# Second cross-attention of a two-layer perceiver block: the first key or value unit of a batch moves between the two halves of the value matmuls

## The reference

```
def _L1_xattn_ref(hidden_states, audio_tokens, attention_mask, Wq, bq, Wk, bk, ...):
    q, k, v = proj(hs, Wq, bq, S), proj(at, Wk, bk, T), proj(at, Wv, bv, T)   # 16 heads of 16 channels
    scores = jnp.clip(jnp.einsum('bhsd,bhtd->bhst', q, k) / scale, -50.0, 50.0)
    scores = jnp.clip(jnp.where(attend, scores, -10000.0), -50.0, 50.0)
    probs = jax.nn.softmax(scores, axis=-1)
    probs = probs / (probs.sum(axis=-1, keepdims=True) + 1e-08)
    ctx = jnp.einsum('bhst,bhtd->bhsd', probs, v)
    delta = _nan_clean(ctx @ Wo.T + bo)
    ...                                        # scaled, layer norm with gamma and beta
x = x + _L1_xattn_ref(_layernorm(x, axis=-1), ctx_2048, mask_BxS2_ik0, ...)
```

## Time and profile before

| what | value |
|---|---|
| time, median of 3 | 647.24 us |
| profiled execution, its own time | 646.73 us |
| its span | 644.9 us |
| TensorE (PE) busy | 632.7 us, 98% of the span |
| PE's weight loads (PEld) busy | 434.5 us, 67% |
| VectorE (DVE) busy | 417.3 us, 65% |
| ScalarE (ACT) busy | 279.8 us, 43% |
| GpSimd (POOL) busy | 59.6 us, 9% |

### The profile page before, as it was taken

How to read it: one execution, slowest core, us unless ns; L and a number is a source line. 1 busy time by engine, 2 the same in 40 slices (tenths; PEclk the granted TensorE clock), 3 DMA queues, 4 the chain that set the end, 5 groups by cost and what they waited for, 6 DMA issues and landing times.

```text
span 644.9 us, 21670 instructions
## 1 busy us (share of the span) xinstructions
PE 632.7 (98%) x9614; PEld 434.5 (67%) x9614; DVE 417.3 (65%) x972; ACT 279.8 (43%) x516; POOL 59.6 (9%) x131
## 2 busy tenths in 40 slices
PE   9999999999999999999999999999999999999996
PEld 5666667667676567666677566767777775456785
DVE  3755467686674755566564672654898965687577
ACT  3454545445353333333443754545445454111156
POOL 1020000000001110111111003200010101000000
PEclk9999999999999999999999999999999999999999
DMA  7242111216105511110012532111235320000001
GB/s 248 67 173 67 36 35 35 67 36 196 36 3 185 177 35 35 34 34 2 2 34 66 135 131 63 68 36 35 71 76 154 133 69 1 2 3 3 4 1 34
DMA packets 28957, 42.25 MB, mean 66 GB/s; under 512 B 6080, under 2 KB 18880, under 8 KB 28352
## 3 DMA queue, kind: packets, MB, share of 16 engines
q1 hardware_dynamic: 28432, 40.47, 19.9%
q10 hardware_dynamic: 432, 0.39, 0.2%
HBM read 40.33 MB, written 0.52 MB: 63 GB/s over the span
## 4 chain that ended last, share of the span: by engine, by line
PE 89%; DVE 8%; issue 1%; ACT 1%; DVEq 0%; POOL 0%; ACTq 0%; POOLq 0%
PE psum L398 17%; PE psum L390 16%; PE psum L1185 7%; PE psum L478 6%; PE psum L443 5%; PE psum L453 4%; PE psum L1161 4%; PE psum L1232 4%; PE psum L2000 2%; PE psum L428 2%; PE psum L1202 2%; PE psum L1977 2%; PE psum L1958 2%; PE psum L1216 1%; DVE arena L2107 1%
## 5 line engine op out<-in xcount | busy, mean ns | idle before, releaser
L398 PE MATMUL psum<-arena 128*128 128x256 f32 x512 | 121.5, 383 | 0.4 <-issue 0.4
L390 PE MATMUL psum<-arena 128*128 128x512 f32 x248 | 117.5, 600 | 0.0
L398 PEld LDWEIGHTS psum<-arena 128*128 128x128 f32 x512 | 93.9, 190 | 22.6 <-issue 10.3
L390 PEld LDWEIGHTS psum<-arena 128*128 128x128 f32 x248 | 43.7, 190 | 41.1 <-issue 39.8
L711 ACT ACTIVATE arena<-arena 128x512 f32<-128x512 f32 x64 | 48.4, 805 | 41.9 <-DVE arena L844 41.9
L1293 ACT ACTIVATE arena<-psum 128x512 f32<-128x512 f32 x48 | 28.4, 597 | 66.2 <-PE psum L1185 37.6
L1185 PE MATMUL psum<-y_cols,arena 128*128 128x512 f32 x112 | 52.1, 599 | 0.0
L705 ACT ACTIVATE arena<-psum,arena 128x512 f32<-128x512 f32 x64 | 40.2, 688 | 27.0 <-DVE arena L831 26.9
L831 DVE TENSOR_REDUCE arena<-psum 128x1 f32<-128x512 f32 x64 | 39.7, 683 | 16.0 <-PE psum L428 15.8
L685 ACT ACTIVATE arena<-psum,arena 128x512 f32<-128x512 f32 x43 | 29.5, 686 | 45.6 <-PE psum L390 41.1
L844 DVE TENSOR_SCALAR arena<-psum 128x512 f32<-128x512 f32 x64 | 39.7, 682 | 11.8 <-PE psum L443 10.8
(11 more groups left out here) (260 smaller groups left out, 953.0 us busy)
## 6 DMA issues: line engine op xcount, KB each, us to landing
arena<-in_ctxT SPq DMA_DIRECT2D x31, 512.0 KB, 3.7
arena<-in_L_attn_Wv SPq DMA_DIRECT2D x1, 2048.0 KB, 8.1
arena<-in_L_attn_Wq SPq DMA_DIRECT2D x8, 256.0 KB, 2.9
arena<-in_L_attn_Wk SPq DMA_DIRECT2D x8, 256.0 KB, 3.6
arena<-in_L_attn_Wo SPq DMA_DIRECT2D x1, 2048.0 KB, 11.6
arena<-in_L_ffn_w_gating SPq DMA_DIRECT2D x1, 2048.0 KB, 7.9
arena<-in_wo_rows SPq DMA_DIRECT2D x2, 1024.0 KB, 5.6
arena<-in_wq_upT SPq DMA_DIRECT2D x2, 768.0 KB, 4.3
```

Source lines behind the costliest of these rows:

```text
L390: last = nc.tensor.matmul(bank, wkv[:, c, i * P:(i + 1) * P], x[:, c, :], start=(c == 0), stop=(c == NC - 1))
L398: last = nc.tensor.matmul(bank[:, kk * D:(kk + 1) * D], x[:, c, k * P:(k + 1) * P], wkv[:, c, D:2 * D], start=(c == 0), stop=(c == NC - 1))
```

## The change

From batch 1 on, the unit of slot 0 is issued after the second of the four value groups, not after the fourth. Batch 0 has no values before it and keeps its order. The wait for the four exponentials (`s_exp`) stays ahead of the first value group; `all_values` is written out in place, and is still called for the last batch.

```diff
     def batch_cols_pe(pe, b):
 
         scores_cols(pe, b, 0), scores_cols(pe, b, 1)
+        between = b > 0
         if b:
-            all_values(pe, b - 1)
+            pe.wait_ge(s_exp, 4 * b)
+            for g in range(G):
+                if g == 2 and between:
+                    unit_pe(pe, slot(b, 0))
+                values(pe, b - 1, g)
         turn_out(pe, tile_at(b, OUT))
-        unit_pe(pe, slot(b, 0))
+        if not between:
+            unit_pe(pe, slot(b, 0))
         turn_taken(pe, tile_at(b - 1, TURN))
         unit_pe(pe, slot(b, 1))
```

## The result

The changed kernel took 650.84 us in the median of four executions (649.53 to 651.57), against 647.01 for the kernel before (646.29 to 647.62). The ratio is 1.0053, with a 95% interval of 1.0038 to 1.0068: slower, by about 3.4 us by the ratio and 3.8 us between the medians. The forecast was 650.4 us, with a range of 649.2 to 651.8. A second series of the same two kernels gave 650.79 to 647.39, ratio 1.0047 (1.0032 to 1.0062).

The account below looks back on a forecast made before the run. The prediction took PE's own time to bound the kernel: 3.63 us of added switches minus 0.47 of gaps gives +3.16, covers costing nothing, so 647.24 + 3.16 = 650.4 us, range 649.2 to 651.8.

Parts of the forecast that it names:

- The bound: Second layer's batches: PE busy 126.90 of 128.00 us, with no wait between engines that an earlier unit could shorten.
- The switches: Batches 1 to 14: added changes between values and full-size work cost 0.27 us in eleven, 0.22 in three, 3.63 in all.
- The first layer's one divided run: First layer's batch 4: values halves of 0.66 us around a unit, against 1.25 whole, priced the split at 0.22.
- The rule that a change of tiling mode drains the engine: Skill rule on PE's mode changes, three a batch becoming five: speaks against the change but gives no price.
- a rival at 652.8: Second layer's batches: all 28 added switches cost 0.20 us each, 5.6 in all; chance 5%.
- The gaps: Issue gaps of 0.55 us in batch 9's values and 0.39 in batch 14's unit: half given back, -0.47.
- the 2.7 that the prediction had as the least: Sign: from batch 1's scores to the fold, second layer, the stretch grows by 2.7 to 3.6 us.
- The rule that the fetch of instructions is mostly hidden: Skill rule on PE's dense values runs: density makes no gap, so no 0.94 us back and a cost of 3.63.
- The covers: Other engines' work stays hidden under PE's: ACT's unit copy 0.96 us ahead of the third unit; cost nothing.
- the late load: Next block's last load before the fold: 0.5 to 1.7 us of room; rival, 0.5 to 1.5 us above the sum, 9%.
- the absorbed: Rival for the second layer's switches: partly absorbed, under +1.3 us of the median, no measurable change; 9%.
- the faster case: Rival: second half's weight loads run under the unit, halves shrink to 0.33 us, kernel takes 645.5; 3%.

Follow-up runs that it names:

- again: The changed kernel once more, with no edit, for a second profile; 650.79 us, ratio 1.0047 to the kernel before.
- unit_ahead: On the kernel before, second layer: slot 0's unit goes wholly ahead of the undivided values run in batches 1 to 14; 648.89 us, ratio 1.0021.
- twice: On the changed kernel: slot 1's unit also goes into the values, ahead of the fourth group, in 13 of 14 batches; 659.31 us, ratio 1.0197.
- shift_half: On the kernel before: 32 small matmuls, results thrown away, once ahead of the second layer's batches (128 more instructions); 649.31 us, ratio 1.0061.
- shift_whole: On the kernel before: 64 small matmuls, results thrown away, once ahead of the second layer's batches (256 more instructions); 648.35 us, ratio 1.0011.
- first_layer_together: On the kernel before, first layer only: values straight behind scores, where a unit stood between, and two units behind the values; 650.85 us, ratio 1.0065.

## Why the prediction was right

**The bound.** Right: PE carries the batches before and after, and no engine's wait was there to be shortened. Only behind batch 15 is VectorE's path as long as PE's: L158 waits 0.2 us for it in executions without a gap there, the second profile of the kernel before among them.

**The switches.** Predicted 3.63 us. Measured in `again` 116.88 - 113.17 = 3.71. The single terms: 0.27 or 0.28 in the common batches, 0.23 in batch 5 (predicted 0.22), 0.27 in batch 6. The first layer's one divided run gave the price for all 14. What it rests on is sharper now: what is paid is the first full-size work behind tiles of another size, behind scores too (`unit_ahead`), and the way into scores costs next to nothing (`twice`, batch 11). What PE does in these 0.20 us no run shows.

**The rule that a change of tiling mode drains the engine** (the Trainium skill, TensorEngine Tiling (Array Packing), section on key properties). Beside it the prediction had a rival at 652.8, with every change at 0.20. It is out: an entry into values costs 0.07 and one into scores at most 0.05. The direction of the rule, that a change costs, holds for the ways out into full-size work.

**The gaps.** This is the term that was mis-sized. I took half of 0.94, so -0.47. The true cost of the two gaps in the kernel before is 1.31 us (8.06 - 7.30 and 8.47 - 7.92), since the chain's rows named issue leave out the slower restart; and the change removed both. The first profile also holds a third gap that the prediction did not count, 0.12 us at 528.27 in the values of batch 15, which the change does not touch. In the first profile of the changed kernel the two are all, a net of 116.94 - 114.48 = 2.46 us in the stretch, less than the 2.7 that the prediction had as the least. In the second a gap of 0.95 comes in batch 15's run behind the scores, which the change left whole: 3.4 us net. The medians, 3.4 to 3.8 us apart, lie at this end, but the intervals of the two series, 2.5 to 4.4 and 2.1 to 4.0 us, do not tell the two cases apart. So that -0.47 came near was luck, two errors that offset: more was given back than I thought, and at least in some executions part of it was taken again in a batch I had not considered. Whether that gap comes in most executions of the changed kernel isn't shown: one profile of two has it.

**The rule that the fetch of instructions is mostly hidden** (the Trainium skill, Runtime: NRT & Kernel Launch, section on instruction fetch mechanics). By it the gaps were not mine to take. In the dense runs the traces disagree: `shift_half` and `shift_whole` show gaps that move with the stream of instructions and return after one block, and in `first_layer_together` they are up to 1.8 us each. Elsewhere the trace agrees: of the 76 blocks in the first profile of the kernel before, four stand ahead of such a gap.

**The covers.** ACT's copy had 1.1 us of room (0.96 predicted), the late load landed at about 527 for a fold at 528.24 (predicted room 0.5 to 1.7 us); neither was reached. `twice` shows that the ACT cover is real and that one more unit ahead of the last quarter is past its end. That the absorbed and the faster case failed was to be expected from the halves of 0.66.

## What to carry to other kernels

On an engine that is already the bound, moving a block into the middle of another kind of work pays the change of tile size once more: price it from a place where the kernel already does it. A run of small matmuls behind other small matmuls can use up instructions faster than they arrive. Its gaps have no releaser in the trace, and each ends shortly after a block of 16 KB has landed on the instruction queue (1.24 to 1.61 us here). They move when anything ahead changes the count of instructions, so a gain or loss of about 1 us after an edit can be theirs and not the edit's. Look at the granted clock behind a long gap, too. Compare the lengths of repeated batches, not spans, since the spans scatter by as much.

## What the runs showed of the hardware that I had not expected

- The gaps named issue wait for instructions. They lie in runs of small matmuls, or in the unit just behind one, where the run stands behind scores, behind 16 transposes (0.27 us in the first layer's last run) or behind the small matmuls of the fold (1.06 in `shift_half`). They last 0.1 to 1.8 us, differ in length between executions of one kernel (0.55 and 0.28 in the same place), moved away with 128 added instructions and came back with 256.
- All 38 of them end 1.24 to 1.61 us after a block of 16 KB has landed on the instruction queue.
- Behind one gap of 1.80 us the granted clock fell from 1.00 to 0.50 for 3.4 us and cost about 1.7 us more; behind gaps of 1.76 and 1.62 us in the same execution it did not.
- A unit of 1.92 us between scores and values was enough to keep them out of all 14 batches (`unit_ahead`, one profile), and a unit inside the run too (two profiles of the changed kernel).
- The first full-size work behind small tiles costs 0.15 to 0.20 us more, while scores (64 rows) behind values (17 columns) cost at most 0.05.
- Spans of the kernel before differ by 1.1 us between two profiles (644.9 and 646.0), and the start of the second layer's batches by 1.2.
